# A cross-attention kernel on one Trainium2 core: the second layer's products in column tiles, and three changes of PSUM bank

## What is computed

```python
# layer 0, 20 heads of 64
n = layer_norm(x);  x = x + attention(n, n)          # 128 keys
n = layer_norm(x);  x = x + attention(n, context)    # 77 keys
x = geglu_ff(layer_norm(x)) + x
# layer 1, 20 heads of 8; of the 77 rows of context 73 are text and 4 image tokens
probs_t = softmax(q @ k_t.T * s)                     # per head 128 x 73
text_out = probs_t @ v_t
qsem = l2norm(probs_t @ text_ehs)                    # its norm comes from the Gram matrix
fused = q @ k_ip.T * s + 0.5 * (qsem @ l2norm(ip).T)
ip_out = (softmax(fused) * mask) @ v_ip
out = (text_out + ip_out) @ W_out + b_out + x
```

## Time and profile before

| | |
|---|---|
| three runs | 3483.93, 3484.61, 3485.42 us, median 3484.61 |
| the profiled execution | 3485.28 us, its span 3483.4 us |
| busy share of the span | PE 96%, PEld 90%, DVE 70%, ACT 66%, POOL 38% |
| granted clock, mean over the span | 0.99 |
| transfers | 90 GB/s in the mean, queue q1 busy 30.5% |

### The profile page before, as it was taken

One profiled execution on the slowest core, in us unless ns is written; L12 is line 12 of the kernel. 1 busy time (PEld: TensorE's weight loads), 2 busy tenths in 40 slices (PEclk: granted clock), 3 DMA queues, 4 the chain that ended last, 5 costly groups with the idle time before them and its releaser, 6 DMA issues. The chain is left out here.

```text
span 3483.4 us, 96098 instructions
## 1 busy us (share of the span) xinstructions
PE 3335.4 (96%) x34878; PEld 3131.8 (90%) x34878; DVE 2438.3 (70%) x7677; ACT 2314.2 (66%) x6485; POOL 1329.5 (38%) x1657
## 2 busy tenths in 40 slices
PE   5899999999999999999999999999999999999997
PEld 4789999999899999999999899998999999899987
DVE  6657677767767767677767767767677776777655
ACT  4566676766767676676766767676676766767654
POOL 2223343333434433343433434433343333434333
PEclk9999999999999999999999999999999999999998
DMA  6432324223142332324223142332324223142310
GB/s 157 157 116 69 105 63 126 74 86 103 54 123 70 108 90 68 108 63 122 78 83 105 54 123 68 106 94 63 113 64 118 82 82 106 54 124 68 94 51 11
DMA packets 210732, 313.84 MB, mean 90 GB/s; under 512 B 31232, under 2 KB 167520, under 8 KB 210272
## 3 DMA queue, kind: packets, MB, share of 16 engines
q1 hardware_dynamic: 209984, 307.53, 30.5%
q10 hardware_dynamic: 288, 0.16, 0.0%
HBM read 267.97 MB, written 14.42 MB: 81 GB/s over the span
## 5 line engine op out<-in xcount | busy, mean ns | idle before, releaser
L997 ACT ACTIVATE SE<-PS,mx 128x77 f32<-128x77 f32 (+1 forms) x2560 | 674.8, 355 | 271.9 <-DVE mx L1248 271.2
L1461 POOL TENSOR_TENSOR SE<-SE,rs 128x512 f32<-128x512 f32 (+1 forms) x640 | 552.7, 869 | 625.7 <-DVE rs L1270 625.7
L1454 POOL TENSOR_TENSOR n<-qq,p_half 128x4 f32<-128x4 f32 x320 | 327.4, 1023 | 987.0 <-DVE qq L1299 987.0
L1265 DVE TENSOR_REDUCE sums<-SE 128x4 f32<-128x512 f32 (+1 forms) x640 | 368.3, 576 | 217.8 <-ACT SE L997 217.3
L985 ACT ACTIVATE PTs<-PT 128x1024 f32<-128x1024 f32 (+1 forms) x320 | 326.5, 1020 | 242.3 <-PE PT L811 240.7
L933 ACT ACTIVATE qk<-PG 128x512 f32<-128x512 f32 (+1 forms) x640 | 326.3, 510 | 127.2 <-PE PG L612 125.5
L773 PE MATMUL PW<-w_o,OTs 128*128 128x160 f32 x2560 | 408.8, 303 | 0.0
L1248 DVE TENSOR_REDUCE mx<-PS 128x8 f32<-128x1024 f32 (+1 forms) x320 | 323.0, 1010 | 115.6 <-PE PS L793 113.4
L827 PE MATMUL PV<-PTs,v_sb 128*64 128x128 f32 (+1 forms) x5120 | 351.1, 279 | 12.3 <-DVE SE L1291 12.0
L773 PEld LDWEIGHTS PW<-w_o,OTs 128*128 128x128 f32 x2560 | 359.7, 191 | 0.0
L876 PE MATMUL PV<-later 73*128 73x86 f32 x2560 | 331.0, 272 | 2.3 <-ACT later L1006 1.4
(11 more groups left out here) (209 smaller groups left out, 8439.1 us busy)
## 6 DMA issues: line engine op xcount, KB each, us to landing
q_slice<-q_split SPq DMA_DIRECT2D x630, 192.0 KB, 2.4
vc_slice<-vc_split SPq DMA_DIRECT2D x155, 512.0 KB, 4.0
kc_slice<-kc_split SPq DMA_DIRECT2D x150, 256.0 KB, 2.9
q1st<-q_hi SPq DMA_DIRECT2D x320, 32.0 KB, 2.1
k1st<-k_hi SPq DMA_DIRECT2D x160, 38.5 KB, 2.2
xres<-in_x_dram SPq DMA_DIRECT2D x32, 160.0 KB, 2.7
q1st<-q_lo SPq DMA_DIRECT2D x160, 32.0 KB, 2.1
out_dram<-x SPq DMA_DIRECT2D x64, 80.0 KB, 1.6
```

The costliest lines, as they stand in the source:

```text
L997: last = a_(SE[:, n % 4, J * i:J * i + J], PS[:, e, J * at:J * at + J], ACT.Exp, bias=mx[:, q % 2, 4 * e + at:4 * e + at + 1])
L1265: v.tensor_reduce(sums[:, n % 2, :], SE[:, n % 4, 0:4 * J].rearrange("p (i j) -> p i j", j=J), AX, ALU.add)\
L1454: gp.tensor_tensor(n20[:, b % 2, 4 * w:4 * w + 4], qq[:, b % 2, 4 * w:4 * w + 4], p_half[:, 0:4], ALU.pow)\
L1461: gp.tensor_tensor(e, e, rs[:, n % 2, :].unsqueeze(2).to_broadcast([128, 4, J]), ALU.mult)\
```

## The change

The code is changed in these places:

- `probs_v1` issues, for each of its four products, two matmuls with 64 of the 128 weight columns each (two column tiles), and writes PT bank 0 in place of PV. It moves from part 2 of its beat to the end of part 0 of the next, right behind `probs_v`, and there waits for `pts_done`.
- `probs_transposed1` writes PV in place of PT bank 0, and moves from the start of part 1 to the end of part 1, behind the jobs. It waits for `ots_done`. On ScalarE `pt1_out` moves along with it, behind `exp` and `qk`, and so stands right ahead of `exp1`.
- On VectorE `unit_out` moves from part 2 to part 1 of the next beat, between the `kc` copy and the second `prob_sums`; `unit_norms` moves from part 0 to part 1, behind the second `prob_sums`, and GpSimd's `norms_of` goes with it. The image branch's steps start one slot later (`tail_slot`), while the slots of their jobs stay.
- The norm's transposes leave the ring PG and go to PS bank 0. They wait for `exp_done`, and the next `scores` wait for `nT_dve`.
- `probs_transposed` waits for `on_done` in place of `pts1_done`, `probs_v` for `pts1_done` in place of `on_done`.
- Behind the last duo, `scores1` alternates between PT bank 1 and PS bank 1.

```diff
         def tail_slot(g, b):
-            return 3 * l1_beat(g, W1 * b + W1 - 1) + 7
+            return 3 * l1_beat(g, W1 * b + W1 - 1) + 8
+        def alone(g, k):
+            return l1_beat(g, k) > DUOS * GROUPS + 1
+        def scores1_bank(g, k):
+            return PS[:, 1, :] if alone(g, k) and k % 2 else PT[:, 1, :]
...
+                def norm_transposed(name, scored):
+                    pe.wait_ge(S["nx_done"], NORM[name[1:]] + 1)
+                    if scored:
+                        pe.wait_ge(S["exp_done"], 2 * scored)
+                    if turned_x[0]:
+                        pe.wait_ge(S["nT_dve"], turned_x[0])
...
@@ probs_transposed
-                    if turned1[0]:
-                        pe.wait_ge(S["pts1_done"], turned1[0])
+                    if product1[0]:
+                        pe.wait_ge(S["on_done"], product1[0])
@@ probs_v
-                    if product1[0]:
-                        pe.wait_ge(S["on_done"], product1[0])
+                    if turned1[0]:
+                        pe.wait_ge(S["pts1_done"], turned1[0])
@@ probs_v1
-                        last = mm(PV[:, GV * i + off:GV * i + off + GS + D1], PTs1[0:TT, 128 * i:128 * i + 128],
-                                  gv[:, b % 2, 2 * w + i // 2, off:off + GS + D1], start=True, stop=True)
+                        for c in range(2):
+                            last = mm(PT[64 * c:64 * c + 64, 0, GV * i + off:GV * i + off + GS + D1],
+                                      PTs1[0:TT, 128 * i + 64 * c:128 * i + 64 * c + 64],
+                                      gv[:, b % 2, 2 * w + i // 2, off:off + GS + D1], start=True, stop=True)
@@ TensorE's loop
                         if duo_at(beat - 1):
                             probs_v(*duo_at(beat - 1))
-                    if part == 1 and l1_at(beat - 1):
-                        probs_transposed1(*l1_at(beat - 1), turned)
+                        if l1_at(beat - 2):
+                            probs_v1(*l1_at(beat - 2), turned)
                     if part == 1 and l1_at(beat):
                         scores1(*l1_at(beat), turned)
                     for name in jobs_at(t)[0]:
                         job(name)
+                    if part == 1 and l1_at(beat - 1):
+                        probs_transposed1(*l1_at(beat - 1), min(max(beat, 0), DUOS * GROUPS))
...
-                    if part == 2 and l1_at(beat - 1):
-                        probs_v1(*l1_at(beat - 1), multiplied)
@@ ScalarE's loop
-                    if sub == 1 and l1_at(beat - 1):
-                        pt1_out(*l1_at(beat - 1))
...
                     if sub == 0 and duo_at(beat - 1):
                         ot_out(*duo_at(beat - 1))
+                    if sub == 1 and l1_at(beat - 1):
+                        pt1_out(*l1_at(beat - 1))
                     if sub == 2 and l1_at(beat):
                         exp1(*l1_at(beat))
@@ VectorE's loop
-                    if sub == 0 and l1_at(beat - 2):
-                        unit_norms(*l1_at(beat - 2))
...
+                    if sub == 1 and l1_at(beat - 2):
+                        unit_out(*l1_at(beat - 2))
                     if sub == 1 and duo_at(beat + 1):
                         g, d = duo_at(beat + 1)
                         prob_sums(g, 2 * d + 1)
+                    if sub == 1 and l1_at(beat - 2):
+                        unit_norms(*l1_at(beat - 2))
...
-                    if sub == 2 and l1_at(beat - 1):
-                        unit_out(*l1_at(beat - 1))
```

More of the change, by code:

```diff
@@ L71, in xattn_program @@
     CTX1_SLOT = {0: 65, 1: 80, 2: 95, 3: 110}
-    TAIL_JOB = {"ipT": 7, "ip": 10, "oT1": 13, "y": 16}
+    TAIL_JOB = {"ipT": 6, "ip": 9, "oT1": 12, "y": 15}
     ctx = ExitStack()
@@ L407, in jobs_at @@
                 first, v = first[:1], v + first[1:]
-            return first + v, [x for x in late_at(t) if x[0] != "v"]
+            return first + v, [x for x in late_at(t) if x[0] not in ("v", "xT")]
         JOBS = [j for t in range(FIRST, LAST) for j in jobs_at(t)[0] + jobs_at(t)[1]]
@@ L672, in job @@
                                           cin[:, b, 128 * c:128 * c + 128], ident[0:TS, 0:TS])
[L673 to L678, removed]
                     elif kind == "qk":
@@ L760, in job @@
                     last.then_inc(S["job_full"], 1)
+                def norm_transposed(name, scored):
[4 more added lines that the diff above has]
+                        pe.wait_ge(S["nT_dve"], turned_x[0])
+                    for part in range(2):
+                        for b in range(HB):
+                            last = tr(PS[:, 0, HT * part + 128 * b:HT * part + 128 * b + 128],
+                                      nx[:, b, 128 * part:128 * part + 128], ident[:, :])
+                    last.then_inc(S["xT_full"], 1)
+                    turned_x[0] = NORM[name[1:]] + 1
                 def wo(g, n):
@@ L882, in _ @@
                     beat, part = divmod(t, 3)
-                    turned, multiplied = min(max(beat + 1, 0), DUOS * GROUPS), min(max(beat, 0), DUOS * GROUPS)
+                    turned = min(max(beat + 1, 0), DUOS * GROUPS)
                     if part == 0:
@@ L896, in _ @@
                         job(name)
+                    if part == 1 and l1_at(beat - 1):
+                        probs_transposed1(*l1_at(beat - 1), min(max(beat, 0), DUOS * GROUPS))
                     if part == 1 and beat > DUOS * GROUPS and l1_at(beat):
                         keep_busy(6)
[L899 to L900 removed]
                     for name in late_at(t):
                         if name[0] == "xT":
[L903 removed]
+                            norm_transposed(name, min(max(beat + 2, 0), DUOS * GROUPS))
                     if part == 2 and duo_at(beat - 1):
@@ L1005, in pt1_out @@
                         act.wait_ge(S["pv1_done"], j - 1)
-                    a_(PTs1[0:TT, :], PT[0:TT, 0, :], ACT.Copy).then_inc(S["pts1_done"], 1)
+                    a_(PTs1[0:TT, :], PV[0:TT, :], ACT.Copy).then_inc(S["pts1_done"], 1)
                 def exp1(g, k):
@@ L1014, in exp1 @@
                     for i in range(4):
-                        last = a_(SE1[:, j % 2, TT * i:TT * i + TT], PT[:, 1, T * i:T * i + TT], ACT.Exp,
+                        last = a_(SE1[:, j % 2, TT * i:TT * i + TT], scores1_bank(g, k)[:, T * i:T * i + TT], ACT.Exp,
                                   bias=mx1[:, j % 2, i:i + 1])
```

41 lines of the change are left out of this document (25 added, 16 removed).

## The result

The changed kernel takes 3676.47 us (median of 4 runs, 3672.19 to 3680.23), the kernel before 3484.42 beside it (4 runs). The ratio is 1.055, with an interval from 1.0532 to 1.0569. That is 192 us slower; the forecast was 74 us slower, and its range ended at 3625. The direction was right, the size was not.

What follows compares the result with a forecast made beforehand. TensorE (PE), busy 96%, was taken to set the pace, with narrow room behind the other engines' results. The sum was 3485.3 - 86 - 30 + 197 - 8 = 3558 us, 2.1% slower, with a range of 3465 to 3625.

Steps and rivals of the forecast that it cites:

- Column tiles, -86: Layer 1's product on PE: eight column-tile pairs take 0.59 us, gaining 0.27 us per beat over 320 beats, -86 us.
- The rival that they don't pay: A pair of column tiles costs what L827's costs, so the product gains 0: 3644 us, chance 0.10.
- a sign with some 190 us: In the profile after, PE's busy time in the product should be near 190 us, from 331 us.
- Waits that go, -30: PE's waits for `on_done`, in the ring and about half of that for GpSimd go, together -30 us.
- New waits, +197: Later work on ScalarE, VectorE and the norm makes new waits of 13.1 us a group, in 15 groups +197 us.
- the one of the last beat: Norm in a group's last beat: the image's exponential comes between and waits for VectorE's L1319, delaying the scores 2.0 us.
- L827's wait for exp1: ScalarE's L1006 stands ahead of exp1, so PE's start behind exp1 comes later: together 1.6 us a group.
- the norms' five: Five of a group's eight norms make the scores wait for the norm's copies: together 5.4 us a group.
- `ff`'s: For two other norms `ff` follows at once and waits for nT: 0.9 us more each, 1.8 together.
- The end, -8: Behind the last duo a second scores bank lets PE run a step ahead: about 16 steps of 0.5 us, -8 us.
- The forecast of too little room between the engines: The room between the other engines' results and PE's use of them is narrow, so moved steps cause new waits.
- The rival "exp1 is in time": ScalarE finishes L1006 without holding exp1 back; new waits are about 5 us a group: 3438 us, chance 0.17.

Runs made afterwards that it cites:

- third buffer: The changed kernel with three SE1 buffers in place of two, so exp1 waits for the `qq_done` of three products before: 3611.85 us, ratio 1.0373.
- The mixed kernel: The 3536.77 us kernel with `unit_out` and `unit_norms` early in beat 4; behind the last duo, `pt1_out` ahead of exp1 and `own_keys` ahead of `norms_of`: 3511.07 us.

## Why the prediction was right and wrong

**Column tiles, -86: right.** The block adds 0.60 us to L843's for the forecast's 0.59, against the old place that is 83 us, and undoing the tiles in the new place costs 98 us in two kernels. The rival that they don't pay is refuted. PE's busy time in the product, given as a sign with some 190 us, is 259.4: the profile counts each block to the modelled end of its last record, 0.77 us in the rows above. By the Trainium skill's overhead of a matmul (TensorEngine Tiling (Array Packing), Performance Considerations), added to each further record, the block would be 0.59 + 0.20 = 0.79 us, an estimate; the trace doesn't agree with such an addition. I wrote that the 0.15 us for leaving column tiles is paid once; that was the point: in the old place it isn't, and there the tiles give nothing.

**Waits that go, -30: about right.** `probs_v` (L843) waits 0.4 us in all where L827 had 12.3, the transposes and L717 no longer wait in the ring, and the wait for GpSimd fell by 14.0 us, about half of 24.4 as said.

**New waits, +197: too small, and the step that failed is the norm's term, "the one of the last beat", together with the clock, which had no term.** The forecast missed by 3676 - 3558 = 118 us: some 88 in the groups and 30 in the end. A group is 11.6 us longer (table) and was counted as 13.1 - 5.4 (tiles) - 2.0 (waits that go) = 5.7 longer. In means over the table's eight groups, beats 19 and 0 make 0.9 + 5.4 = 6.3 of the 11.6 (beat 0 is shorter in some groups, so its mean increase is below the 6.04 of the medians), where the count had 2.0 - 0.5 (tiles) = 1.5. All others together make 5.3, where it had 4.2.

The term had 2.0 us for beat 19, made of the image's exponential behind L1347. Missing was that exp1 itself waits for `qq_done`. I had moved `unit_norms` behind the second sums and asked what queues behind it on VectorE and GpSimd, but not who waits for its own semaphore. That wait stands in the function `exp1` and the change doesn't touch it; it has 86.8 us and 141 times in ACT's list. With a third buffer 65 us come back.

That the other beats came near the count is in part luck. The third buffer makes them 2.1 us a group shorter as well, mostly beats 4, 5, 6 and 9, by a wait that the count did not hold. Single terms differ too: L827's wait for exp1 was put at 1.6 us a group and is 45.2/15 = 3.0, the norms' five were put at 5.4 and are 4.3, `ff`'s was put at 1.8 and grew by (52.2 - 17.1)/15 = 2.3.

**The clock was not in the sum at all.** The forecast charged a wait with its own length. In beat 0, 1.6 us of waiting cost 4.4 us more by PE's low level (with the 12 matmuls: 10.87, without: 15.31). Of the 192 us up to 83 are the clock's share. No row of before had a fall in a group to take a price from, but the earlier trace rows showed the clock at 1.00, with room to fall.

**The end, -8: wrong in sign.** It went from 127.8 to 150.1 us, +22. Up to 19 of them are the clock's share, 37 us in place of 18; how much of that is on the path of the end was not measured. The steps in a trace of the end are bound by the ring of waits L864, maxima, `unit_out`, L1327, GpSimd's powers, the spreading of the keys, L864:

```profile
3599.54 0.46 DVE L1327 TENSOR_REDUCE qq<-SE 128x4 f32<-128x292 f32 x1
...
3600.08 1.01 POOL L1482 TENSOR_TENSOR n<-qq,p_half 128x4 f32<-128x4 f32 x1 [4.13 <-DVE qq L1327]
...
3601.05 0.70 POOL L1499 TENSOR_TENSOR kbd<-k1st,head_of_row 96x308 fp32r<-96x308 f32 x1
3601.89 0.38 PE L864 MATMUL PT<-kbd,q1st 96*128 96x308 f32 x1 [1.42 <-POOL kbd L1499]
```

The keys of the next step are spread behind `norms_of`, which waits for L1327. I had named the second bank's gain and left GpSimd's queue out. GpSimd's order alone gets 10 of the 22 us back (140.1). The mixed kernel, with GpSimd's and ScalarE's order changed there, gets 14 of the 16 us that are left in the kernel it is made from, to 130.2; the two orders were not tried apart there. That a second bank lets the scores run ahead was not tested by itself.

**The sum of the rest.** With a third buffer and two changes of order (VectorE's and ScalarE's) the kernel goes from 3676.47 to 3536.77: 140 of 192 us were waits that the change's order and its two buffers made, up to 76 of them by the clock's share (118 to 3532.7 x 0.012 = 42). What stays is 52 us: 2.3 us a group, 35 in all, and 16 in the end. The longest new wait in it is L827's behind `unit_out` (61.9 us, set against the tiles' gain). The forecast of too little room between the engines was right. The rival "exp1 is in time" is refuted by L827's 48 waits behind exp1.

## What to carry to other kernels

When a step is moved, search every wait on the semaphores that it signals, in the functions the change leaves alone too: who waits for this step, not only who queues behind it. An edit to an order has no price of its own: putting one copy behind exp1 cost 56 us while exp1 waited for another engine, and a move of the same copy, behind exp1 and the copy to nT, gained 49 once it didn't. A wait of PE can cost more than its length, so look at the granted clock behind it. Column tiles pay next to a block in the same tiling; alone between full-width blocks their two borders can cost what they save.

## What the runs showed of the hardware

The granted clock is 1.00 from 1980.00 to 1993.00, with a wait of 1.07 us before L827 at its end. It falls to its low level in the wait of 1.66 us before L809 (1993.72 to 1995.38), and is back at full some 10 us later:

```profile
1994.00:1995.00 1.00, 0.00 (x0) 0.00 (x0) 0.58 (x2) 1.00 (x3) 1.00 (x2) 0.97 0.22 53
1995.00:1996.00 1.00, 0.62 (x6) 0.65 (x8) 0.97 (x5) 0.56 (x1) 0.07 (x1) 0.50 0.51 157
...
2005.00:2006.00 1.00, 1.00 (x10) 1.00 (x10) 0.96 (x4) 0.15 (x1) 0.33 (x1) 0.91 0.18 44
```

The beat runs at 0.67 in the mean, which at levels of 1.0 and 0.5 is 15.31 x 0.33 x 2 = 10.1 us at the low one, four times the 2.7 us of waiting. The same two waits do not always cost as much: beat 0 takes 15.0 to 15.5 us in 11 of the 14 groups that have them, and 12.5 to 12.8 in three. Filling the second wait with 12 matmuls that compute nothing kept the clock up in that beat and gained 42 us in all. The Trainium skill (TensorE: Matmul & The Clock Gate, Part 1: The HAM clock gate) puts the ramp penalty, which it gives for a kernel's warm-up, below 1% of a typical span. This case is another one, since most falls come in the middle of the run: here the clock's share is 118 of 3676 us, 3.2% of the span.

A block of matmuls in two column tiles costs 0.09 us more to enter and some 0.15 us to leave among full-width blocks. L843 takes 0.92 us until the tiled product behind it starts, and 1.03 until a full-width one does.
